# Cross-attention with a quantised FFN on one Trainium2 core: another order of the last stage's projections and turns, and two-source forms of its small VectorE operations

## The reference

```python
# x (8, 1024, 512), context (8, 2048, 512), mask (8, 2048); 16 heads of 32
xn = layer_norm(layernorm(x), g1, b1);  cn = layer_norm(context, g2, b2)
q, k, v = xn @ Wq.T, cn @ Wk.T, cn @ Wv.T
attn = softmax(where(mask, q k^T / sqrt(32), -inf))
x = x + (attn v) @ Wo.T + bo
y = layernorm(x)
# FFN: y and its weight are quantised in blocks of 32 along the features:
scales = max(max|block| / 7.5, 1e-30);  q = nearest value of the FP6 E2M3 grid to block / scales
x = x + (yq * ys) @ (wq * ws).T + bias
```

## Time and profile before

| | |
|---|---|
| median of the runs | 4335.55 us |
| profiled execution, its own time | 4338.36 us |
| its span | 4336.6 us |
| granted TensorE clock, mean | 0.998 |
| TensorE matmul busy | 97% |
| VectorE busy | 80% |
| ScalarE busy | 66% |
| GpSimd busy | 68% |
| mean DMA traffic | 125 GB/s |

### The profile page before, as it was taken

One profiled execution on the slowest core, in us unless ns is written; L12 is line 12 of the kernel. 1 busy time (PEld: TensorE's weight loads), 2 busy tenths in 40 slices (PEclk: granted clock), 3 DMA queues, 4 the chain that ended last, 5 costly groups with the idle time before them and its releaser, 6 DMA issues.

```text
span 4336.6 us, 87951 instructions
## 1 busy us (share of the span) xinstructions
PE 4204.9 (97%) x36752; PEld 1392.0 (32%) x35088; DVE 3454.3 (80%) x3960; ACT 2857.8 (66%) x5193; POOL 2938.9 (68%) x1830
## 2 busy tenths in 40 slices
PE   4999999999999999999999999999999999999999
PEld 2322243222532234222342223422234222342223
DVE  5689767887678976888768897688976899768986
ACT  3388843888438875488755886558865588646885
POOL 3199752996529965399644996449963599536994
PEclk9999999999999999999999999999999999999999
DMA  5256652666426574265733567335664356643664
GB/s 201 73 118 128 141 172 64 121 124 152 158 61 124 120 185 131 61 129 117 205 109 70 118 127 195 104 75 121 125 190 109 80 118 125 185 113 78 122 131 117
DMA packets 191558, 541.68 MB, mean 125 GB/s; under 512 B 29025, under 2 KB 103073, under 8 KB 148786
## 3 DMA queue, kind: packets, MB, share of 16 engines
q0 software_dynamic: 43776, 318.79, 36.7%
q1 hardware_dynamic: 147378, 217.27, 16.2%
HBM read 119.37 MB, written 22.05 MB: 33 GB/s over the span
## 4 chain that ended last, share of the span: by engine, by line
PE 76%; DVE 8%; POOL 6%; DMA 5%; ACT 3%; issue 2%; SPq 0%; DVEq 0%; ACTq 0%; POOLq 0%
PE banks L1212 18%; PE banks L1111 18%; PE banks L1224 17%; PE banks L1175 7%; PE banks L1179 5%; DVE max_parts L689 5%; PE banks L1255 4%; PE banks L1105 4%; POOL wkT_wvT_wqT L474 3%; PE banks L1080 3%; DMA sums<-wkT_wvT_wqT 3%; ACT region L979 2%; POOL wdT L474 1%; DMA region<-in_x 1%; DMA wdT<-wkT_wvT_wqT 1%
## 5 line engine op out<-in xcount | busy, mean ns | idle before, releaser
L689 DVE TENSOR_REDUCE max_parts<-banks 128x2 f32<-128x1024 f32 x2048 | 2403.3, 1219 | 364.9 <-PE banks L1175 340.8
L979 ACT ACTIVATE region<-banks 128x512 f32<-128x512 f32 x4096 | 2190.1, 610 | 428.9 <-PE banks L1212 360.8
L474 POOL TENSOR_TENSOR wkT_wvT_wqT<-region 128x1024 f32<-128x1024 f32 x528 | 1353.4, 2776 | 451.6 <-ACT region L979 341.1
L1212 PE MATMUL banks<-queries_stacked,keys_stacked 98*32 98x512 f16 x16384 | 1270.4, 382 | 13.3 <-ACT values L963 6.2
L1224 PE MATMUL banks<-region,values 128*32 128x512 f32 x8192 | 1080.2, 600 | 19.1 <-ACT region L979 15.5
L1212 PEld LDWEIGHTS banks<-queries_stacked,keys_stacked 98*32 98x32 f16 x16384 | 403.4, 95 | 1168.0 <-ACT region L979 770.5
L1111 PE MATMUL banks<-region,wkT_wvT_wqT 128*128 128x512 f16 x2304 | 558.0, 381 | 15.1 <-DMA wkT_wvT_wqT<-weights_split 12.8
L1175 PE MATMUL banks<-keys_stacked,queries_stacked 33*128 33x512 f16 x2432 | 475.1, 387 | 6.8 <-DVE max_parts L689 3.5
L474 POOL TENSOR_TENSOR sums<-region 128x1024 f32<-128x1024 f32 x144 | 386.1, 2826 | 0.2 <-ACT region L979 0.2
L454 POOL TENSOR_TENSOR region<-row_sums_inverse,region 128x512 f16<-128x512 f32 x80 | 93.1, 1163 | 432.5 <-ACT region L942 431.8
L1111 PE MATMUL banks<-wkT_wvT_wqT,region 128*128 128x512 f16 x1536 | 368.8, 380 | 0.0
(11 more groups left out here) (108 smaller groups left out, 3354.0 us busy)
## 6 DMA issues: line engine op xcount, KB each, us to landing
wdT<-wkT_wvT_wqT POOLq DMA_DIRECT2D x96, 1024.0 KB, 12.0
wkT_wvT_wqT<-wkT_wvT_wqT POOLq DMA_DIRECT2D x80, 1024.0 KB, 7.5
sums<-wkT_wvT_wqT POOLq DMA_DIRECT2D x72, 1024.0 KB, 7.5
wkT_wvT_wqT<-sums POOLq DMA_DIRECT2D x40, 1024.0 KB, 7.6
wkT_wvT_wqT<-weights_split SPq DMA_DIRECT2D x8, 3072.0 KB, 20.8
keys_stacked<-region SPq DMA_DIRECT2D x384, 64.0 KB, 2.0
keys_stacked<-sums SPq DMA_DIRECT2D x384, 64.0 KB, 2.0
region<-in_x SPq DMA_DIRECT2D x16, 1024.0 KB, 8.3
```

Source lines behind the costliest of these rows:

```text
L474: e.tensor_tensor(SUMS[dst][:, half], PR[i][:, half], PR[i + 1][:, half], ALU.add).then_inc(s_pr, 1)
L689: e.tensor_reduce(mpart[:, buf, :, a, t, c], MXB[parity], AX.X, ALU.max).then_inc(s_mxd, 1)
L979: e.activation(PR[u % 4][:, j * HALF:j * HALF + HALF], score_bank(m % NU, kt, j)[0], ACT.Exp, scale=SCALE).then_inc(s_ex, 1)
L1212: mm = e.matmul(dst[HD * t:HD * t + HD, :], KA[0:STR, ds(ka + (j * C + (u + 1) * P + HD * t), HD)], QA[0:STR, ds(qa[j], HALF)], start=True ...
```

## The change

Three things change. The small operations of the scales (L866) and of the variances of four tiles (L604, L606) get the form `scalar_tensor_tensor`, whose second source is a small constant tensor; GpSimd sets the three constants at the start. TensorE projects tile `k + 4` ahead of turning tile `k`, for `k < 4`. The next tokens' statistics, their inverse deviations and their centring come two tiles later on VectorE, GpSimd and ScalarE.

```diff
-    NEXT_AT = (2, T // P - 1)
+    NEXT_AT = (4, T // P - 1)
...
+        least = sb("least_scale", [P, NB], F32)
+        eps_once, eps_twice = (sb(f"eps_{n}", [P, 4], F32) for n in ("once", "twice"))
...
+        s_le = sem("least_values_set")
...
+            for t, value in ((least, FP8_STEP * SCALE_MIN), (eps_once, EPS), (eps_twice, EPS * EPS)):
+                e.memset(t[:, :], value).then_inc(s_le, 1)
...
                 ch.settle()
-                if twice:
-
-
-                    e.tensor_scalar(var, mean_var[:, :, 1], 1 + EPS, EPS * EPS, ALU.mult, ALU.add).then_inc(s_ve, 1)
+                if var.shape[1] == 1:
+                    e.tensor_scalar(var, mean_var[:, :, 1], EPS, None, ALU.add).then_inc(s_ve, 1)
                 else:
-                    e.tensor_scalar(var, mean_var[:, :, 1], EPS, None, ALU.add).then_inc(s_ve, 1)
+                    e.scalar_tensor_tensor(var, mean_var[:, :, 1], 1 + EPS if twice else 1.0,
+                                           (eps_twice if twice else eps_once)[:, :], ALU.mult, ALU.add).then_inc(s_ve, 1)
...
+            e.wait_ge(s_le, 3)
             e.wait_ge(s_wf, 48)
...
-                    ch.did(e.tensor_scalar(scale64[i % 2][:, :], amax[:, :], FP8_STEP / FP6_MAX, FP8_STEP * SCALE_MIN,
-                                           ALU.mult, ALU.max))
+                    ch.did(e.scalar_tensor_tensor(scale64[i % 2][:, :], amax[:, :], FP8_STEP / FP6_MAX, least[:, :],
+                                                  ALU.mult, ALU.max))
...
-                    if 1 <= i <= NEXT_AT[0]:
+                    if NEXT_AT[0] - 1 <= i <= NEXT_AT[0]:
                         next(parts[0], None)
...
-                    if i in (4, 5) and b + 1 < B:
-                        centred(0, (i - 4) * 2, 2)
+                    if NEXT_AT[0] < i <= NEXT_AT[0] + 2 and b + 1 < B:
+                        centred(0, (i - NEXT_AT[0] - 1) * 2, 2)
...
                 for k in range(TT):
                     if k < LEAD:
+                        out_project(k + LEAD)
                         turn_quantised(k)
-                        out_project(k + LEAD)
```

## The result

The changed kernel takes 4348.51 us (median of 10 runs, 4345.54 to 4350.85), the kernel before 4338.06 us (10 runs, 4334.62 to 4341.01). The ratio is 1.0025, with a 95% interval of 1.0015 to 1.0035: 10.5 us slower, between 6.5 and 15.2. The forecast was 15.6 us slower, 4351.2 us in all. The profiled executions took 4348.81 us (span 4346.9) and 4338.36 us (span 4336.6).

The account below looks back on a forecast made before the run. TensorE, busy 97% of the span, was taken as the bound. Seven inner stages (13.0 us) plus the last batch (2.6) gave 15.6 us more: 4335.55 + 15.6 = 4351.2 us, range 4338 to 4359 for 8 in 10 runs.

Parts of the forecast that it names:

- The exposed copy: First three tiles of a last stage: TensorE's ffn waits for ScalarE's copy of the turned tile, a gap of 0.94 us.
- F0: Tile 0's ffn on TensorE, 8 matmuls; claimed to begin 1.28 us after that tile's turn began, against 0.44 in a full queue.
- T0: Turn of tile 0 on TensorE, four transposes; claimed at 12.95 us after the stage's start, its 1.56 us stop gone.
- Tile 5's chain: From tile 3's turn through ScalarE, VectorE and GpSimd to tile 5's turn: 6.10 us, making TensorE wait 1.29.
- T5: Turn of tile 5 on TensorE, four transposes; claimed at 41.25 us after the stage's start, after a wait.
- Rival (C): Last stages: tile 5's turn doesn't wait, tile 6's follows 3.87 later; 57.31 us a stage, 4338.4 us, no change; chance 0.14.
- T6: Turn of tile 6 on TensorE, four transposes; claimed at 45.44 us after the stage's start, also in the last batch.
- The forms: VectorE's two-source small operations: no saving counted beside GpSimd, long cases stay; if they escaped, at most 1.1 us per case.
- Rival (B): Tile 5's scale on VectorE meets GpSimd, costing up to 1.0 us in each of eight stages: 4359 us; chance 0.10.
- The statistics: Next tokens' statistics moved later on VectorE, with GpSimd and ScalarE work: hidden, 0 us, bounds -0.2 and +0.5 per stage.
- The stage of before: Inner last stage of the old kernel, taken as 57.06 us; the new 58.92 is 1.86 more, seven times 13.0.
- Rival (D): First tiles of a last stage: the copy doesn't hold the ffn; stage 54.0 us, 23.7 us faster, 4311.8; chance 0.05.

## Why the prediction was right or wrong

**The exposed copy: right.** F0 started 1.28 after T0, as taken. The shown length of F grew from 3.60 to 3.70 and its step from 3.43 to 3.54, the first load of weights that can't be made early. The gap is 0.84 + 0.11 = 0.95; 0.94 was taken.

**Tile 5's chain: right, but not the only one.** T5 came 6.12 after T3, 6.10 was taken. The wait was real but not by itself the price. The forecast put y(3) "right behind" quantise(5) at 4.96 and noted that F3 ends at 4.81, but did not take that end for a second bound. Rival (C) therefore had T6 follow T5 by 3.87 once T5 doesn't wait. With T5's wait removed alone, T6 didn't move. Rival (C)'s 57.3 us a stage needed both ways cut, and then came out at 57.32.

**The forms: right.** No saving, long cases kept, ratio 1.0000 alone. Rival (B) didn't happen: tile 5's scale took 0.18 at 584.48, 1.6 us after GpSimd's last L557 had ended (2.2 had been worked out).

**The statistics: right for the new order, with less room than worked out.** They were put at "0, bounds -0.2 and +0.5 per stage". The order alone costs 10.5 us and so does the whole change. Maxima(4) was to start at 29.72, with 0.2 to spare; in the first stage it starts at 30.40, since the variance of four tiles ahead of it (L609) took 1.26 us beside GpSimd's L557. T4 has the room and doesn't wait.

**The stage of before: the term that was mis-sized.** The new stage was forecast at 58.92 and took 59.05, and the last batch's T6 was right too. But the sum subtracts the stage of before as one profile has it, 57.06, and the last batch's T6 at 42.83. In the next profile of the same kernel the mean stage is 403.4 / 7 = 57.63 and that T6 is at 43.78; in that of the forms alone, with the old order and place, it is 57.71 and 44.08. The load and L720 had been short in the first one. Against the second profile the stages lose 413.6 - 403.4 = 10.2 us and the last batch 60.1 - 58.4 = 1.7: 11.9, and the spans differ by 4346.9 - 4335.6 = 11.3. Both have two falls of the clock. Against the first it is 14.2 + 2.6 = 16.8, near the 15.6 forecast, but the spans differ by only 10.3, mainly since that profile had three more falls (5.1 us). That the ten timed runs of before are like the second profile is argued from these three, not shown run by run.

The place of the statistics hides in this. "That stop goes, but O5 to O7 don't need it" was said of the load's wait, and no cost of it in the old stage was looked for. There it reaches T1 and the tiles behind, and moving the statistics alone gives 5.4 us. The new order takes the same time back by its gaps, so the two gains don't add: the order costs about 15 us with the statistics late and 10.5 with them early.

**Luck.** The forecast of 4351.2 us lies 2.7 from the measured 4348.51, the difference of 15.6 lies 5.1 from the measured 10.5. The three runs that it started from had a median of 4335.55, the ten have 4338.06, and this error went the other way.

**Rival (D)** didn't happen in this change: the copy holds F, by the gap above. Its 54.0 us a stage was right as TensorE's own work.

## What to carry to other kernels

In an in-order queue, ask what stands between an instruction's producer and its consumer on another engine. Moving one independent block ahead of both saves its stop once and exposes the round trip every time. When a wait is removed and nothing moves, look for a second path of the same length, often a sum or a store-side operation queued ahead of the next tile's work. And price a change against more than one profile: here the mean stage of before varied by 0.6 us, with the arrival of a load and with one VectorE operation beside GpSimd, and the change makes both harmless.

## What the runs showed of the hardware

A VectorE operation of 16 values with two sources in SBUF was held by GpSimd's `tensor_tensor` just as the one-source form was (1.28 us beside 0.18). With two sources of 512 elements (L720) it took 0.69 to 1.57 us in the two profiles of before, and where it was held it ended 0.55 us after GpSimd's. The operation of one value per partition took 0.15 to 0.16 us throughout, also in the 49 cases in which it lay wholly beside a long GpSimd `tensor_tensor` in the two kernels with the scales on ScalarE. The scales took ScalarE 307 to 309 ns each, over all 64. TensorE's clock fell to its lower level in or just behind stops of 3.2 to 3.9 us in the last stage, in six of eight stages; stops of 3.1 and 2.7 us in the other two had no fall. It also fell at the start of the attention after stops of under 1 us, in none to five of the eight batches.
